# Two expert layers of a transformer kernel: norms moved into the attention, places counted on TensorE, rows gathered per expert

## What is computed

```python
x = x + _L0_xcond_ref(_layernorm(x), ctx_1024, ...)
x = x + _L0_ffn_ref(_layernorm(x), ...)      # norms once more inside
...
x = x + _L3_xcond_ref(_layernorm(x), ctx_1024, ...)
x = x + _L3_ffn_ref(_layernorm(x), ...)

def _L3_ffn_ref(x, Wg, W1, b1, W2, b2):
    gates = softmax(xf @ Wg.T);  topw, topi = top_k(gates, 2)
    C = int(round(K * T * CAP_RATIO / E))            # 538 places per expert
    cnt = number of earlier choices of the same expert, all first choices ahead of all second ones
    within = cnt < C
    buf[e, cnt] = the token's row                     # only where within
    h = gelu(buf @ W1 + b1);  y = h @ W2 + b2
    out[token] = sum over its 2 choices of topw * within * y[e, cnt]
```

## Time and profile before

| | us |
|---|---|
| median of 3 runs | 2799.79 (2796.5 to 2806.28) |
| profiled execution, its own time | 2800.2 |
| its span, first to last instruction | 2798.4 |
| TensorE busy | 2245.9 (80%) |
| VectorE busy | 1929.3 (69%) |
| ScalarE busy | 1271.8 (45%) |
| GpSimd busy | 1130.9 (40%) |
| mean granted TensorE clock | 0.893 |

### The profile page before, as it was taken

One profiled execution on the slowest core, in us unless ns is written; L12 is line 12 of the kernel. 1 busy time (PEld: TensorE's weight loads), 2 busy tenths in 40 slices (PEclk: granted clock), 3 DMA queues, 4 the chain that ended last, 5 costly groups with the idle time before them and its releaser, 6 DMA issues. The chain is left out here.

```text
span 2798.4 us, 83518 instructions
## 1 busy us (share of the span) xinstructions
PE 2245.9 (80%) x36280; PEld 1553.3 (56%) x36376; DVE 1929.3 (69%) x4359; ACT 1271.8 (45%) x2309; POOL 1130.9 (40%) x834
## 2 busy tenths in 40 slices
PE   6834938644699999999999989999999999788182
PEld 3523824323366666666666666666666666554172
DVE  4461225576799888988898988888989898444311
ACT  2311303252356656554656555656565656233030
POOL 0004050000376565656555655665556565200304
PEclk9956968866799999999999999999999999789586
DMA  7102010000011121112111211121111111300022
GB/s 253 41 2 61 28 41 1 1 0 0 27 33 29 33 60 32 37 33 60 32 37 32 59 33 37 33 60 32 37 32 29 32 37 33 108 2 2 20 66 59
DMA packets 71859, 110.86 MB, mean 40 GB/s; under 512 B 11394, under 2 KB 56712, under 8 KB 64966
## 3 DMA queue, kind: packets, MB, share of 16 engines
q1 hardware_dynamic: 67398, 97.88, 12.6%
q0 software_dynamic: 4096, 7.63, 0.9%
HBM read 42.29 MB, written 16.78 MB: 21 GB/s over the span
## 5 line engine op out<-in xcount | busy, mean ns | idle before, releaser
L2583 POOL TENSOR_TENSOR mem<-mem 128x512 f32<-128x512 f32 x384 | 572.6, 1498 | 606.7 <-DVE mem L2142 589.7
L1865 PE MATMUL ps<-mem 128*128 128x512 f32 x768 | 396.2, 620 | 3.8 <-DVE mem L2142 1.3
L2422 ACT ACTIVATE mem<-ps 128x512 f32<-128x512 f32 x384 | 219.6, 601 | 226.6 <-PE ps L1886 226.1
L2401 ACT ACTIVATE mem<-ps 128x512 f32<-128x512 f32 x384 | 228.7, 600 | 162.6 <-PE ps L1865 121.7
L2137 DVE TENSOR_TENSOR mem<-ps,mem 128x512 f32<-128x512 f32 x384 | 258.7, 674 | 22.5 <-ACT mem L2401 22.4
L2142 DVE TENSOR_TENSOR mem<-ps,mem 128x512 f32<-128x512 f32 x384 | 260.9, 679 | 0.0
L1886 PEld LDWEIGHTS ps<-mem 128*128 128x128 f32 x1536 | 186.4, 144 | 122.7 <-issue 104.3
L1947 PEld LDWEIGHTS ps<-mem 64*64 64x64 f32 x12288 | 193.3, 136 | 79.4 <-issue 77.2
L1874 PE MATMUL ps<-mem 128*128 128x512 f32 x384 | 207.2, 623 | 31.5 <-ACT mem L2461 19.2
L2149 DVE TENSOR_REDUCE mem<-mem 128x16 f32<-128x1024 f32 x192 | 231.8, 1207 | 0.0
L2596 POOL TENSOR_TENSOR mem<-mem 128x1024 f32<-128x1024 f32 x96 | 182.3, 1899 | 100.6 <-DVE mem L2211 100.6
(11 more groups left out here) (281 smaller groups left out, 4129.2 us busy)
## 6 DMA issues: line engine op xcount, KB each, us to landing
mem<-mem SPq DMA_DIRECT2D x48, 768.0 KB, 5.8
mem<-in_Wqkv SPq DMA_DIRECT2D x6, 1536.0 KB, 6.9
mem<-mem SPq DMA_DIRECT2D x36, 256.0 KB, 3.5
x<-mem SPq DMA_DIRECT2D x10, 512.0 KB, 6.5
mem<-x SPq DMA_DIRECT2D x16, 320.0 KB, 5.6
y<-mem SPq DMA_DIRECT2D x16, 320.0 KB, 2.5
mem<-in_W12T SPq DMA_DIRECT2D x8, 512.0 KB, 7.3
mem<-in_L3W SPq DMA_DIRECT2D x16, 256.0 KB, 5.1
```

The costliest lines, as they stand in the source:

```text
L1865: e.matmul(self.K.ps[:, o, :], self.columns(u, bb), self.K.l2[l % 2]["Wqkv"][:, 512 * i:512 * i + 512], start=True, stop=True, skip_group_ ...
L2401: e.activation(self.SQ[:, 512 * j:512 * j + 512], self.K.ps[:, self.ROTATE[i], :], ACT.Square).then_inc(s("squared"), 1)
L2422: e.activation(to, view(self.K.ps[:, self.FEATURE[i], :], "p (c q) -> p c q", c=4), ACT.Copy).then_inc(s("placed"), 1)
L2583: e.tensor_tensor(t1[:, cols], t1[:, cols], self.T2[:, cols], ALU.add).then_inc(s("rotated"), 1)
```

## The change

It has five parts.

1. The norms ahead of an expert layer are given to the attention before it: once a batch's two windows are added, its 24 steps join the generator. While that is so, `fill` after a maximum takes six steps instead of three. Batch 2's norm is done in one go after window 6, batch 3's after the attention's last addition. The constants that attention 0 prepared at its end are prepared two rounds earlier.
2. The first layer's two norms are one: with variance v and eps, norming twice is the same as one norm whose root is taken of v (1 + eps) + eps squared.
3. TensorE turns and routes batch by batch. VectorE does softmax and best choices for the first twelve tiles while batch 3 is still normed, turned and routed, then for the last four.
4. Places are counted in PSUM: a bf16 product with the lower triangle and then one product with ones for each shift of the tiles, 16 in all (32 in the last layer, where second choices come behind all first ones). VectorE's doubling steps go.
5. Rows are gathered and not scattered. SyncE stores the normed rows of each batch as they are. A place is split into column (of 40, five per expert) and low part (of 128); 32 products of one-hots give for each place the row of its token, and 40 indirect gathers, five per expert, bring the rows. The zeros and their ten stores go.

```diff
+            if self.last and q == self.NQ - 2:
+                self.last(e)
...
-                    self.fill(3)
+                    self.fill(6 if self.norms else 3)
...
+                if self.norms and w % 2 == 0:
+                    self.extra = chain(self.extra, self.norms(e, w // 2 - 1, s.at("added", w)))
+                    if w + 2 == self.NW:
+                        self.fill(999)
...
-        if self.last:
-            self.last(e)
+        self.fill(999)
...
+                t = v(e.tensor_scalar(a, eps[0], 1.0 + eps[1], eps[1] * eps[1], ALU.mult, ALU.add))
...
-        for k in ("x0", "x3"):
-            for j in range(E * SLOTS // 1024):
-                e.dma_start(K.slots[k][1024 * j:1024 * j + 1024, :].rearrange("(t p) d -> p t d", p=128),
-                            view(K.zeros, "p (t d) -> p t d", d=D)).then_inc(K.s["zero"], 16)
...
+        for n, z in enumerate((slice(0, NT - 4), slice(NT - 4, NT))):
+            e.wait_ge(*s.at("routed", (B - 1, B)[n]))
+            self.v_softmax(e, n, z)
+            self.v_best(e, z)
         self.v_places(e)
...
+        e.tensor_tensor(self.col_hot, columns, bc(col, 2, 5 * E), ALU.is_equal).then_inc(s("col_hot"), 1)
+        for z in (slice(0, 9), slice(9, 18), slice(18, 2 * NT)):
+            e.tensor_tensor(self.low_hot[:, z], slots(z.stop - z.start), bc(low[:, z], 2, 128), ALU.is_equal).then_inc(s("low_hot"), 1)
+        e.wait_ge(*s.at("index", 1))
+        K.v(e.tensor_copy(self.fetch, ps[:, 1, 0:5 * E]))
...
+        self.pe_turn(e, 0)
         for b in range(B):
...
+            if b + 1 < B - 1:
+                self.pe_turn(e, b + 1)
+            self.pe_route(e, b)
+            if b == B - 2:
+                self.pe_turn(e, b + 1)
...
+        last = e.matmul(to, K.lowerb, hot, start=True, stop=False, skip_group_check=True)
+        for t in range(1, NT):
+            last = e.matmul(to[:, :, E * t:n], K.ones3, hot[:, :, 0:n - E * t], start=False, stop=t == NT - 1,
+                            skip_group_check=True)
+        if self.k_major:
+            for t in range(NT):
+                last = e.matmul(view(to[:, 1], "p (t e) -> p t e", t=NT), K.ones3, bc(self.oh[:, 0, t, :], 1, NT), start=False,
+                                stop=t == NT - 1, skip_group_check=True)
...
+        e.activation(self.col_ids[:, :, 0], self.col_hot, ACT.Copy, scale=self.K.row).then_inc(s("col_rows"), 1)
...
+        e.tensor_tensor(view(self.col_ids[:, :, 1], "p (k t) c -> p k t c", k=2),
+                        view(self.col_hot, "p (k t) c -> p k t c", k=2), tiles, ALU.mult).then_inc(s("col_tiles"), 1)
+        e.wait_ge(*s.at("rows_stored", 16 * B))
+        e.wait_ge(*s.at("indexed", 1))
+        fetch = self.fetch.bitcast(U32)
+        for x in range(E):
+            for j in range(5):
+                m = min(128, self.cap - 128 * j)
+                e.indirect_dma_start(self.xe[0:m, x, j, :], None, xs,
+                                     bass.IndirectOffsetOnAxis(fetch[0:m, 5 * x + j:5 * x + j + 1], 0),
+                                     bounds_check=B * S - 1, oob_is_err=False).then_inc(s(f"xe{x}"), 16)
...
-        e.wait_ge(*s.at("put", 512))
-        for x in range(E):
-            e.dma_start(self.xe[:, x], xs[SLOTS * x:SLOTS * x + SLOTS, :].rearrange("(t p) d -> p t d", p=128)
-                        ).then_inc(s(f"xe{x}"), 16)
+        for b in range(B):
+            e.wait_ge(*s.at("ready_rows", 4 * b + 4))
+            e.dma_start(xs[S * b:S * b + S, :].rearrange("(t p) d -> p t d", p=128), K.XN[:, 4 * b:4 * b + 4, :]
+                        ).then_inc(s("rows_stored"), 16)
```

More of the change, by code:

```diff
@@ L130, in __init__ @@
         self.lenB = words(B)
-        self.idx = words(L)
+        self.idx = words(128)
+        self.row = words(1)
+        self.columns = words(5 * E)
+        self.lowerb = words(64).bitcast(BF16)
         self.sel3 = words(3)
@@ L203, in root_steps @@
         if eps is not None:
-            t = v(e.tensor_scalar(a, eps[0], eps[1], None, ALU.add))
+            if twice:
+                t = v(e.tensor_scalar(a, eps[0], 1.0 + eps[1], eps[1] * eps[1], ALU.mult, ALU.add))
+            else:
+                t = v(e.tensor_scalar(a, eps[0], eps[1], None, ALU.add))
             yield
@@ L871, in v_places @@
-        v(e.scalar_tensor_tensor(pos, fits, -16384.0, pos, ALU.mult, ALU.add))
-        e.wait_ge(v.sem, v.n)
-        e.tensor_scalar(self.put.bitcast(I32), pos, 16384.0, None, ALU.add).then_inc(s("placed"), 1)
-        e.wait_ge(*s.at("placed", 1))
+        hot = e.tensor_tensor(view(oh, "p k t e -> p (k t) e"), bc(K.iota8, 1, 2 * NT), bc(flat(ixf), 2, E), ALU.is_equal)
+        if self.k_major:
+            hot.then_inc(s("one_hot"), 1)
+        else:
+            t = v(hot)
+            e.wait_ge(v.sem, t)
+            e.tensor_tensor(self.both, oh[:, 0], oh[:, 1], ALU.add).then_inc(s("one_hot"), 1)
@@ L1018, in __init__ @@
         self.weights_loaded = K.s["moe0"], 256
-        self.normed = lambda b: self.s.at("rows", 8 * (b // 2) + 8)
     def place_memory(self):
@@ L1025, in extra_memory, with norm_steps @@
         self.sg = [self.K.m.words(320) for _ in range(3)]
-    def v_norm(self, e):
-        K = self.K
-        K.layernorm(e, K.X, K.XN, self.s("first_norm"))
-        K.layernorm(e, K.XN, K.XN, self.s("rows"), ready=self.s.at("first_norm", NT))
-    def v_columns(self, e, b):
-        pass
+    def norm_steps(self, e, b, ready):
+        K, s = self.K, self.s
+        yield from K.norm_steps(e, K.X, K.XN, b, s("ready_rows"), ready, twice=True)
     def a_columns(self, e, b):
@@ L1128, in extra_memory, with norm_steps @@
         pass
-    def v_norm(self, e):
-        self.K.layernorm(e, self.K.X, self.K.XN, self.s("rows"))
-    def v_columns(self, e, b):
-        pass
+    def norm_steps(self, e, b, ready):
+        yield from self.K.norm_steps(e, self.K.X, self.K.XN, b, self.s("ready_rows"), ready)
     def a_columns(self, e, b):
@@ L2834, in declare @@
     out = nc.dram_tensor("out_x", (B * S, D), F32, kind="ExternalOutput").ap()
[L2835 removed]
+    slots = {k: nc.dram_tensor(k, (B * S if k[0] == "x" else E * SLOTS, D), F32, kind="Internal").ap()
+             for k in ("x0", "y0", "x3", "y3")}
     return d, kept, slots, out
```

247 lines of the change are left out of this document (132 added, 115 removed).

## The result

Before 2803.03 us (median of 4 runs, 2796.5 to 2806.4), after 2766.51 us (4 runs, 2758.4 to 2775.9), on one chip: ratio 0.987, 95% interval 0.984 to 0.990. The kernel became faster by 1.3%, not by the 3.6% forecast; 2766.5 lies outside the range of 2688 to 2724. The profiled execution has a span of 2765.1.

A forecast was written before the change was run, and what follows sets the result against it. Bound by two uncovered holes ahead of the expert layers, 99.0 and 83.8 us, where one engine works at a time. Terms -60.0 - 43.4 + 4.2 - 1.0 = -100.2 gave 2700 us from 2800.2; range 2688 to 2724.

The forecast's parts named there:

- Terms 1 and 2: From T0 (end of VectorE's last attention addition) to the first expert's transposes, first and last layer: -60.0 and -43.4 us.
- products do not overlap: Rival: bf16 products in the counting chains and row table cost about 0.31 us each; total 2723; 8%.
- the passes block each other: Rival: GpSimd's multiply for the place-to-row table comes behind all three VectorE compares; +4.3 us per layer, 2709; 22%.
- Term 3: Last layer's experts: TensorE waits 2.7 us for the third expert's rows, plus 1.5 for lost clock; +4.2.
- Term 4: Attentions take over norm steps and lose one of TensorE's two norm waits: about -0.5 us each, -1.0 together.
- T0 itself moves by more than 5: Sign of a wrong prediction: the end of VectorE's last attention addition shifts by over 5 us.
- an expert of the first layer that waits for its rows: Sign of a wrong prediction: gathers, 6.55 us per expert, were to keep ahead of first-layer transposes 12.4 apart.
- gathers are slow: Rival: experts' gathers take g us each, over 1.31, starving experts of rows; g = 3.5 gives 2820 (3%), 1.9 2713 (6%).

The follow-up runs named there:

- spread: Changed kernel, each empty place reading a row of its own instead of row 0: 2696.93 us (chip 12), 2758.25 (chip 10), 2697.01 (chip 3, rows from a loaded table).
- chip 3 kernel that reads row 0 in both layers: Spread version with the rows for empty places loaded as a constant table, here row 0 for all of them in both layers: 2700.41 us.
- the paced one: Changed kernel, GpSimd waiting before expert x's gathers (x from 2) until expert x-2's rows are turned: 2700.27 us (chip 12), 2709.55 (chip 10).
- a control: Same instructions as the spread version, one constant changed so that all empty places read row 0 again: 2761.98 us, ratio 0.988, on chip 14.

## Why the prediction was wrong

**Terms 1 and 2, the holes: right to 2 us.** -58.2 and -41.9 for -60.0 and -43.4. Batch 3's norm ends at T0 + 4.7 (4.8 foreseen), the last route at 11.6 and 11.6 (12.4), the one-hot at 16.5 (17.4). The count took 1.1 and 3.7 us (2.0 and 3.8): in chains, bf16 products pay no fixed price, so the rival "products do not overlap" is out. The first gather starts at T0 + 30.9 and 32.9 (31.1, 32.5); the turns come at 40.8 and 41.9 (39.0, 40.4). Of the 1.8 and 1.5 too little the slow transfers of empty places make 1.2 and 1.0: spread, the turns come at 39.6 and 40.9 (chip 3).

Inside this term two errors cancel. The work ahead of the compares ended 1.7 earlier than counted (first layer), and "the passes block each other" did happen, in another order than the rival had. In order of time the three compares took 1.35, 3.49 and 2.01. By source, the compares before and after 168.5 (count, shortest/median/longest in ns), and GpSimd's multiply:

```profile
L898 DVE TENSOR_TENSOR mem<-mem x1: 1351/1351/1351, 167.4 to 167.4; 128x1152 bf16<-128x1152 f32 x1
```

```profile
L898 DVE TENSOR_TENSOR mem<-mem x2: 2010/2751/3492, 168.6 to 172.1; 128x1152 bf16<-128x1152 f32 x1, 128x1792 bf16<-128x1792 f32 x1
```

```profile
L1031 POOL TENSOR_TENSOR mem<-mem 128x1280 bf16<-128x1280 bf16 x1 | 3.4, 3385 | 21.3 <-DVE mem L896 21.3
```

Two compares of one size take 1.35 and 3.49. The multiply starts at 167.54 and ends at 170.92; if it waits for the first compare to end at 168.73 it works 2.2 us (2.3 foreseen), and the second compare waits for it and then needs 1.2 to 1.35. So they ran one after the other. This is the rule of the Trainium skill, SBUF — State Buffer, section on the two separate sides: whichever of the two starts first has the shared port for its whole instruction, and the other waits. The trace agrees with 3.49 against 1.35. I had taken the overlap. It cost 2.1 of VectorE's time per layer, and not 4.3, since GpSimd came second and not last. The other rule of the Trainium skill on that page and in that section, on GpSimd's DMAs held up beside a VectorE copy within SBUF, was hardly put to the test: g stayed 1.30, but the experts' VectorE work beside the gathers reads PSUM.

**Term 3, TensorE waits for the third expert's rows: the size was off.** +4.2 foreseen, of which 2.7 waiting. From the first to the last turn of the last layer the chip 3 kernel that reads row 0 in both layers takes 57.8 against 55.0, +2.8; but it waits only 0.2 for the second expert's rows and 0.5 for the third's, since its first expert came late itself. 1.3 of the 2.8 was not foreseen: each later expert takes 9.19 instead of 8.94. With spread rows on the same chip the waits are 0.9 and 1.7, and the third turns come 12.8 after the first (13.1 foreseen).

**Term 4, the attention: the size was off, not the mechanism.** One wait for VectorE's norm in place of two, as foreseen, but from 2.6 to 3.9:

```profile
PE ps L276 <- DVE mem L257: 3.9, 1, 3.9
```

From the first to the last addition, attention 0 took 90.6 before; in the 19 profiles with the change 84.1 to 91.6, most near 85.5; the last attention 89.2, and 84.1 to 90.8, most at 85.6. So it is about -5 and -3.6 where I had -0.5 each. Yet the changed kernel's own last attention took 85.6 in the first comparison and 90.8 on chip 10, with the same wait of 4.0 in both and a granted clock of 0.93 and 0.87: the clock moves it by as much as the whole gain. Before had 0.89 and 0.91 in its two attentions, so with one profile of it I can't split the gain between the wait and the clock. By the prediction's own sign (T0 itself moves by more than 5) it was wrong here too: T0 came 6.0 earlier, at 145.8; its other sign, an expert of the first layer that waits for its rows, did not appear.

**What failed is the rival "gathers are slow".** It was the right place and the wrong mechanism. I asked only what a gather costs the one who needs its rows (g), and put the price of their length at nothing as long as "none waits". g was as computed to 0.01 us, and TensorE waited for rows only at the start and, by 0.3, for the third expert of the last layer. What the step left out is that a stream of gathers can slow engines that wait for nothing in it: 33.4 and 34.4 us in the two layers. That rival stood at 3% for g = 3.5 (2820), and no rival gave 2766.

The whole sum on a chip that does not starve (row 0 read in both layers, span 2701.9), in the stretches of the table above: 147.7, 41.0, 86.9, 2251.2, 42.0, 57.8, 75.2. Without starving the forecast of 2700 holds: 2700.41. That it does so within half a us is luck: the attentions gave more than term 4, term 3 cost less, the holes gave less, and the stretch between the two layers, in which the change touches little but the last attention, takes from 2240.4 to 2258.0 in the profiles of the versions. With starving, 33.4 and 34.4 us come back, of which 2.8 is term 3: 65 of the 100.

**What is settled, and what is not.** Shown: the 65 us belong to starving; it takes an unbroken stream of the gathers that fetch the experts' rows (waits that break the stream take back 49 us on the same chip); which rows are read plays no part, neither on chip 3, where nothing starves, nor on chip 10, where both versions do; the same kernel starves on one chip and not on another.

A long stream alone is not enough. Every kernel here has a second one in each expert layer: the 32 gathers that bring the results back, 1.30 apart for 41 us, which no version paced. In the last layer, the changed kernel of the first comparison, and then the kernel of chip 3 that reads row 0 in both layers:

```profile
2715.93 1.03 POOL L1049 DMA_INDIRECT mem<-y,mem  x1 [72.78 <-issue]
...
2738.21 2.31 DVE L1074 SCALAR_TENSOR_TENSOR mem<-mem 128x128 f32<-128x128 f32 x8 [8.21 <-DMA mem<-y,mem]
```

```profile
2652.66 1.03 POOL L1052 DMA_INDIRECT mem<-y,mem  x1 [40.88 <-issue]
...
2674.97 2.31 DVE L1077 SCALAR_TENSOR_TENSOR mem<-mem 128x128 f32<-128x128 f32 x8 [8.23 <-DMA mem<-y,mem]
```

VectorE's additions start 22.3, 32.7 and 43.3 us into this stream in the first and 22.3, 32.8 and 43.3 in the second: in a profile whose engines starve beside the other gathers, nothing is late here. The engines have little to do beside this stream, TensorE almost nothing, and it reads another buffer. Which of these differences matters wasn't tried.

"Chip" here stands for chip and moment: each chip was used at one time only, so a neighbour's work or something set at start-up can't be told from the chip itself. Every execution here was also recorded by the profiler, so whether its records take part is not known. Not tried on a chip that starves: plain transfers from SyncE or GpSimd. So whether it takes indirect ones is open, and with it the mechanism: the traces show instructions late one by one, inside a group that waits for no semaphore too. Late instruction fetches are not what they show. In the queue that by the counts serves TensorE, 199 of its loads and products lie between the last fetch before the starved stretch and the next one, and 199 between the same two fetches of the unstarved kernel that reads row 0 (chip 3). In the changed kernel this next fetch comes at 242.7, when TensorE has been back at its usual pace for some 8 us.

**The version to use** is the paced one, which is faster than both kernels: 2700.3 on chip 12 and 2709.6 on chip 10, ratios 0.964 and 0.970, against 2759.0 of the changed kernel on chip 10 (and 2766.5 in the first comparison). Waits that also bind at the start of the last layer, and pacing with spread rows, weren't run.

## What to carry to other kernels

When an engine's work is declared hidden because nobody waits for its result, ask too what it does to the others while it runs; here a 52 us stream of GpSimd's gathers beside the experts took back two thirds of the gain. Break such a stream into pieces that are asked for by their users. And compare versions on one chip only, then repeat the winner on another: an interval of 0.3% from one chip said nothing of the 2.3% between two, and a control that ran on another chip than the kernel it controls nearly proved a false cause.

## What the runs showed of the hardware

- With GpSimd issuing gathers 1.30 apart without a break, TensorE, VectorE and ScalarE slowed down to one instruction in 0.7 us or more, from 16 to 24 us after the stream's start until 2 to 6 us after its end: on chips 14 and 10 and in the first comparison in all 7 profiles with at least 30 of the experts' gathers in a row, on chips 12, 8 and 3 in none of 6. After a pause of 7.7 us it took 12 us of the new stream. The 32 gathers of the results, 1.30 apart too, delayed nothing in the same profiles.
- Indirect gathers that read one row up to 128 times: in the first layer of the changed kernel 166 of 640 packets of 4 KB took over 0.5 us, up to 2.1; with rows of their own (chip 3) all stayed under 0.5, the middle one at 0.21. The spacing of the gathers did not change.
- GpSimd issues a plain transfer in 0.53 us (40 in 21.4), an indirect one in 1.30.
- A VectorE compare with two inputs in SBUF and a GpSimd multiply run one behind the other: 1.35 us alone, 3.49 behind the multiply.
